# Part 2 of a two-part transformer block: experts weighted by pairs on VectorE and summed in a tree on GpSimd, with new orders on three engines

## The reference

```python
rw = _gating(hidden_states, sim_matrix, gates)            # [b, t, 16], a weight for each expert
q = jnp.einsum('bte,bted->btd', rw, jnp.einsum('btc,ecd->bted', hidden_states, q_proj))
k = jnp.einsum('bte,bted->btd', rw, jnp.einsum('btc,ecd->bted', hidden_states, k_proj))
v = jnp.einsum('bte,bted->btd', rw, jnp.einsum('btc,ecd->bted', hidden_states, v_proj))
scores = where(causal, jnp.einsum('bqd,bkd->bqk', q, k) * scale, -inf)
attn = jnp.einsum('bqk,bkd->bqd', jax.nn.softmax(scores, axis=-1), v)
mixed = attn[:, :, None, :] * rw[..., None]
return jnp.einsum('bted,edc->btc', mixed, o_proj)
```

## Time and profile before

| | before |
|---|---|
| median of 3 runs | 1579.34 us (1577.45 to 1579.94) |
| the profiled execution's own time | 1579.77 us |
| its span (first to last instruction) | 1577.8 us |
| TensorE busy, whole span | 1406.7 us, 89% |
| VectorE busy | 1044.1 us, 66% |
| ScalarE busy | 846.3 us, 54% |
| GpSimd busy | 467.7 us, 30% |

### The profile page before, as it was taken

One profiled execution on the slowest core, in us unless ns is written; L12 is line 12 of the kernel. 1 busy time (PEld: TensorE's weight loads), 2 busy tenths in 40 slices (PEclk: granted clock), 3 DMA queues, 4 the chain that ended last, 5 costly groups with the idle time before them and its releaser, 6 DMA issues.

```text
span 1577.8 us, 55685 instructions
## 1 busy us (share of the span) xinstructions
PE 1406.7 (89%) x24914; PEld 1044.7 (66%) x24914; DVE 1044.1 (66%) x1599; ACT 846.3 (54%) x1753; POOL 467.7 (30%) x496
## 2 busy tenths in 40 slices
PE   1599999999999999999999999999963687878876
PEld 0257777777777777777777777777762355555555
DVE  5576666766766666676766667676317577777776
ACT  2056565565655655665556556556633345545543
POOL 4202323233343323324232333412232222222221
PEclk9689999999999999999999999999985899999999
DMA  3101010110101001010110101010002000000000
GB/s 102 45 17 43 7 38 19 27 33 13 43 13 33 23 23 35 11 43 13 33 24 22 43 3 43 13 33 3 3 8 48 2 6 8 8 6 9 8 8 10
DMA packets 37037, 36.43 MB, mean 23 GB/s; under 512 B 14272, under 2 KB 24256, under 8 KB 36800
## 3 DMA queue, kind: packets, MB, share of 16 engines
q1 hardware_dynamic: 36288, 32.62, 8.7%
q10 hardware_dynamic: 512, 0.26, 0.1%
HBM read 5.33 MB, written 2.10 MB: 5 GB/s over the span
## 4 chain that ended last, share of the span: by engine, by line
PE 76%; DVE 9%; POOL 6%; issue 4%; ACT 4%; SPq 1%; DMA 0%; DVEq 0%; POOLq 0%; ACTq 0%
PE att_ps L511 31%; PE st_ps L495 15%; PE ring_ps L562 14%; PE ring_ps L549 4%; POOL sum_P L470 3%; PE qkv_ps L645 3%; POOL sum_P L473 2%; DVE part L1253 2%; PE ring_ps L542 2%; PE ring_ps L583 2%; DVE part_max L1078 1%; PE ring_ps L575 1%; ACT by_A L899 1%; DVE nm L1299 1%; PE t_ps L688 1%
## 5 line engine op out<-in xcount | busy, mean ns | idle before, releaser
L1078 DVE TENSOR_REDUCE part_max<-ring_ps 128x2 f32<-128x1024 f32 x512 | 625.5, 1224 | 353.3 <-PE ring_ps L562 344.4
L511 PEld LDWEIGHTS att_ps<-v_sb,pT 128*64 128x64 f32 x16384 | 632.2, 138 | 145.4 <-issue 30.1
L511 PE MATMUL att_ps<-v_sb,pT 128*64 128x65 f32 x16384 | 651.1, 222 | 2.4 <-issue 2.4
L799 ACT ACTIVATE pT<-st_ps 128x512 f32<-128x512 f32 x1024 | 553.8, 608 | 160.8 <-PE st_ps L495 153.8
L495 PE MATMUL st_ps<-qa,ka 98*64 98x512 f16 x2048 | 398.4, 387 | 0.0
L562 PE MATMUL ring_ps<-ka,qa 96*64 96x512 f16 x2048 | 313.5, 386 | 27.6 <-DMA ka<-split 19.1
L645 PE MATMUL qkv_ps<-ew_split,x2T 128*128 128x384 f16 x768 | 156.9, 337 | 25.7 <-issue 18.8
L807 ACT ACTIVATE raw_attn<-att_ps 128x260 f32<-128x260 f32 x128 | 49.5, 387 | 205.7 <-PE att_ps L511 205.7
L495 PEld LDWEIGHTS st_ps<-qa,ka 98*64 98x64 f16 x2048 | 115.4, 110 | 61.2 <-issue 10.2
L562 PEld LDWEIGHTS ring_ps<-ka,qa 96*64 96x64 f16 x2048 | 96.5, 113 | 66.5 <-issue 33.1
L470 POOL TENSOR_TENSOR sum_P<-by_A 128x576 f32<-128x576 f32 x32 | 44.9, 1404 | 256.1 <-ACT by_A L899 256.1
(11 more groups left out here) (193 smaller groups left out, 1310.8 us busy)
## 6 DMA issues: line engine op xcount, KB each, us to landing
qa<-split SPq DMA_DIRECT2D x192, 64.0 KB, 2.0
ka<-split SPq DMA_DIRECT2D x192, 64.0 KB, 2.0
resid<-in_L_attn_x SPq DMA_DIRECT2D x4, 512.0 KB, 7.3
out<-yo SPq DMA_DIRECT2D x32, 64.0 KB, 1.5
qa<-shift_rows ACTq DMA_DIRECT2D x64, 4.0 KB
wkv_sb<-in_L_attn_Wkv SPq DMA_DIRECT2D x1, 512.0 KB, 5.3
ew<-in_L_ffn_q_proj SPq DMA_DIRECT2D x1, 512.0 KB, 5.8
ew<-in_L_ffn_k_proj SPq DMA_DIRECT2D x1, 512.0 KB, 7.6
```

The costliest lines, as they stand in the source:

```text
L511: mm = pe.matmul(att_ps[q0:q0 + TILE_COLS, qt * DV1:(qt + 1) * DV1], pT[:, blk % 2, kt, qt * P + q0:qt * P + q0 + TILE_COLS], v_sb[:, j % ...
L799: act.activation(pT[:, blk % 2, kt, :], st_ps[:, c % ST_BANKS, :], ACT.Exp).then_inc(exp_ok, 1)
L1078: dve.tensor_reduce(part_max[:, which % 2, 2 * quarter + m // 2, m % 2, :], pair.rearrange("p (n k) -> p n k", n=2), AX.X, ALU.max, negate ...
```

## The change

VectorE no longer chains. For a pair it does one tensor_tensor over 2 x 192 elements: the PSUM bank times the two weights, broadcast, into a new SBUF tensor `prod[P, 2, 16, 192]`, which takes ScalarE's products too. GpSimd adds all sixteen in place: 4 + 4 experts (768 elements) three times, then 384, then 192 into `qkv`. The chain, `part`, `by_A`, `sum_P` and together(m) go. The order of steps changes on TensorE, ScalarE and VectorE, and the waits on `rest_ps` with it.

```diff
@@ GpSimd
             for m in range(B * NT):
-                pool.wait_ge(weighted_A, 2 * len(PAIRS_A) * (m + 1))
+                into = prod[:, m % 2, :, :]
+                pool.wait_ge(weighted_A, 6 * m + 4)
+                pool.wait_ge(weighted_V, 5 * m + 2)
+                pool.tensor_tensor(into[:, 0:4, :], into[:, 0:4, :], into[:, 4:8, :], ALU.add).then_inc(added_P, 1)
+                pool.wait_ge(added_P, OPS_P * m + 1)
+                pool.wait_ge(weighted_A, 6 * (m + 1))
+                pool.wait_ge(weighted_V, 5 * m + 3)
+                pool.tensor_tensor(into[:, 0:4, :], into[:, 0:4, :], into[:, 8:12, :], ALU.add).then_inc(added_P, 1)
+                pool.wait_ge(added_P, OPS_P * m + 2)
+                pool.wait_ge(weighted_V, 5 * (m + 1))
+                pool.tensor_tensor(into[:, 0:4, :], into[:, 0:4, :], into[:, 12:16, :], ALU.add).then_inc(added_P, 1)
+                pool.wait_ge(added_P, OPS_P * m + 3)
+                pool.tensor_tensor(into[:, 0:2, :], into[:, 0:2, :], into[:, 2:4, :], ALU.add).then_inc(added_P, 1)
+                pool.wait_ge(added_P, OPS_P * m + 4)
                 if m >= 2:
-                    pool.wait_ge(weighted_V, OPS_V * (m - 1))
-                pool.tensor_tensor(sum_P[:, m % 2, :, :], by_A[:, m % 2, 0:3, :], by_A[:, m % 2, 3:6, :], ALU.add).then_inc(added_P, 1)
-                for n in (1, 2):
-                    pool.wait_ge(added_P, 3 * m + n)
-                    pool.tensor_tensor(sum_P[:, m % 2, 0, :], sum_P[:, m % 2, 0, :], sum_P[:, m % 2, n, :], ALU.add).then_inc(added_P, 1)
+                    pool.wait_ge(v2_ok, m - 1)
+                    pool.wait_ge(lo2, 2 * (m - 1))
+                pool.tensor_tensor(qkv[:, m % 2, :], into[:, 0, :], into[:, 1, :], ALU.add).then_inc(added_P, 1)
@@ TensorE: outputs(m), qk_transposes(m), values2(m)
                 if live(m + 1):
                     pe.wait_ge(mx_ok, m + 2)
+                if live(m + 2):
+                    pe.wait_ge(qkt_ok, m + 3)
...
-                if live(m - 2):
-                    pe.wait_ge(mx_ok, m - 1)
+                if live(m - 1):
+                    pe.wait_ge(mx_ok, m)
...
-                if live(m + 1):
-                    pe.wait_ge(qkt_ok, m + 2)
+                pe.wait_ge(qkt_ok, m + 1)
@@ TensorE: order of a step
                 outputs(m - 4)
                 project(m, 0)
                 project(m, 1)
+                project(m, 2)
+                p_transposes(m - 2)
+                project(m, 3)
+                project(m, 4)
+                values2(m - 2)
+                project(m, 5)
                 qk_transposes(m - 1)
-                p_transposes(m - 2)
-                project(m, 2)
+                m_transposes(m - 3)
+                project(m, 6)
                 scores2(m - 1)
-                project(m, 3)
-                values2(m - 2)
-                project(m, 4)
-                m_transposes(m - 3)
-                for pair in (5, 6, 7):
-                    project(m, pair)
+                project(m, 7)
@@ ScalarE: high_parts(m) and the order of a step
-                act.wait_ge(weighted_V, OPS_V * (m + 1))
+                act.wait_ge(added_P, OPS_P * (m + 1))
...
+                weighted(m, 0)
+                weighted(m, 2)
+                p_copy(m - 2)
                 high_parts(m - 1)
-                weighted(m, 0)
+                weighted(m, 4)
                 qk_copy(m - 1)
-                p_copy(m - 2)
-                weighted(m, 2)
+                m_copy(m - 3)
                 softmax2(m - 1)
-                weighted(m, 4)
-                m_copy(m - 3)
@@ VectorE: weighted(m, pair) and the order of a step
+                if pair == PAIRS_V[0] and m >= 2:
+                    dve.wait_ge(added_P, OPS_P * (m - 1))
+                dve.tensor_tensor(prod[:, m % 2, 2 * pair:2 * pair + 2, :],
+                                  qkv_ps[:, (8 * m + pair) % QKV_BANKS, 0:6 * DE].rearrange("p (e d) -> p e d", e=2),
+                                  rw_all[:, m, 2 * pair:2 * pair + 2].unsqueeze(2).to_broadcast([P, 2, 3 * DE]),
+                                  ALU.mult).then_inc(weighted_V, 1)
...
-                low_parts(m - 1)
                 add_tokens(m - 4)
                 weighted(m, 1)
                 p_copy(m - 2)
-                maxima2(m - 1)
                 weighted(m, 3)
+                low_parts(m - 1)
                 mixed(m - 2)
                 weighted(m, 5)
                 m_low(m - 3)
                 weighted(m, 6)
+                maxima2(m - 1)
                 weighted(m, 7)
-                together(m)
```

More of the change, by code:

```diff
@@ L56 @@
 PAIRS_V = (1, 3, 5, 6, 7)
-OPS_V = 2 * len(PAIRS_V) + 1
-CHAIN_V = ((0, None), (0, 0), (0, 1), (0, 2), (0, 3), (0, 4), (1, None), (0, 5), (1, 6), (0, 7))
+OPS_P = 5
 EARLY = 3
@@ L202, in block_kernel @@
         eow_split = sb("eow_split", [P, 2, E // 2, C], F16)
-        by_A = sb("by_A", [P, 2, 2 * len(PAIRS_A), 3 * DE])
-        sum_P = sb("sum_P", [P, 2, 3, 3 * DE])
-        part = sb("part", [P, 2, 3 * DE])
+        prod = sb("prod", [P, 2, E, 3 * DE])
         qkv = sb("qkv", [P, 2, 3 * DE])
@@ L642, in project @@
                     else:
-                        pe.wait_ge(weighted_V, OPS_V * then + 2 * (PAIRS_V.index(of) + 1))
+                        pe.wait_ge(weighted_V, len(PAIRS_V) * then + PAIRS_V.index(of) + 1)
                 for k, (x_part, w_part) in enumerate(SPLIT_PRODUCTS):
@@ L896, in weighted @@
                     if m >= 2:
-                        act.wait_ge(added_P, 3 * (m - 2) + 1)
+                        act.wait_ge(added_P, OPS_P * (m - 1))
                 for e in (2 * pair, 2 * pair + 1):
-                    act.activation(by_A[:, m % 2, 2 * PAIRS_A.index(pair) + e % 2, :], expert_out(m, pair, e), ACT.Copy,
+                    act.activation(prod[:, m % 2, e, :], expert_out(m, pair, e), ACT.Copy,
                                    scale=rw_all[:, m, e:e + 1]).then_inc(weighted_A, 1)
```

## The result

The changed kernel takes 1629.08 us (median of 4, 1624.65 to 1629.97), the one before 1578.39 us in the same comparison: ratio 1.0315, 95% interval 1.0293 to 1.0336. It is slower by about 50 us, as forecast in direction and inside the range; the forecast of 1612 us is 17 us short. The profiled execution took 1624.65 us, with a span of 1622.7 us; before it was 1577.8 us.

A forecast was written before the change was run, and what follows sets the result against it. No engine is full; a ring of waits around the engines bounds each tile. Start +2.9, periods +27.9 and tail -2.6 make +28.2 us, 1607.5 us as a median; +5 us for TensorE's clock gives 1612 us, range 1597 to 1634.

The forecast's parts named there:

- The ring: Waits once around the engines, through weighted(7), GpSimd's last adds, low_parts, mixed and the q and k transposes; mean 10.47 us.
- the hold: On VectorE, low_parts' first instruction is blocked until GpSimd's running first add ends: 1.15 us more in each tile.
- 9.71 + d: Tile period in us if low_parts are not blocked; d is maxima2's time, 0.29 (v = 0) to 1.225 (v = 7).
- The port: VectorE instructions with two SBUF inputs wait for GpSimd's add to end; low_parts blocked, 1.15 us a tile, mean period 11.6.
- The first rival: GpSimd's add does not block low_parts on VectorE: -8.2 us, 1571 us; chance 0.10.
- TensorE's clock: Idle 3.0 to 3.7 us ahead of the q and k transposes, about one in four tiles begins at 1.2 GHz: +5 us.
- Q: Start of a tile's three transposes of q and k on TensorE, the mark for periods; before, 10.63 us apart.
- The second rival: TensorE's clock falls in every tile: 1607.5 + 23 = 1631 us; chance 0.12.
- my own case: low_parts blocked by GpSimd's first add, some tiles begun at 1.2 GHz: between 1598 and 1624 us; chance 0.71.
- The third rival: weighted(m, 3) comes over 1.1 us later, so low_parts go before GpSimd's first add: 1575 to 1590 us; chance 0.05.
- Start and tail: Up to the q and k transposes of tile 2, +2.9 us; from those of tile 31 to the end, -2.6 us.
- The fourth rival: VectorE is the bound, and its 1.75 us less in a tile gives -56 us, 1524 us; chance 0.02.

The follow-up runs named there:

- e2b_port_fill: The changed kernel with GpSimd's first add waiting for low_parts and pair 5 projected four times over: 1576.31 us, 0.9992 of the kernel before.
- e1_port: The changed kernel with one wait more, GpSimd's first add of a tile waiting for low_parts of the tile before: 1579.88 us.
- e3_add: The kernel before with one more GpSimd add of 768 elements in each tile, on spare SBUF that nobody reads: 1649.17 us.
- e3_memset: The kernel before with one more GpSimd instruction in each tile, a memset of 2304 elements on spare SBUF: 1577.88 us.
- e2_fill: The changed kernel with pair 5 of each tile but the first projected six times over, same result: 1608.56 us.
- e4_orders: The kernel before with the change's new orders and waits on TensorE, ScalarE and VectorE, but the old sums: 1546.69 us.
- e6_short: The changed kernel with GpSimd's first add waiting for low_parts and a tree whose last adds are small: 1547.70 us.

## Why the prediction was right, and where it was short

1. **The ring and its period without the hold, 9.71 + d: right.** e2b_port_fill has 10.12 to 11.06 against 10.00 to 10.94, 0.12 us more in each tile. Of this, 0.09 us is the way from weighted(7) to `qkv`, 3.71 us for 3.62. Prices of all new instructions were within 1.5%.
2. **The port: right, and shown from both sides.** Taken away in the changed kernel (e1_port), put alone into the kernel before (e3_add), and without GpSimd's reads (e3_memset). Size: 1.10 us a tile for 1.15 (the prediction's own terms, 2.34 and 1.17, give 1.17). This error and that of the ring run against each other, so that a tile with the hold came within 0.08 us of the forecast was in part luck.
3. **The first rival** (port not held, 1571) is refuted as a forecast by L1259; as a reckoning of a kernel without the hold it was near (1576 in e2b_port_fill).
4. **TensorE's clock: the term that was mis-sized.** The prediction let one in four of 29 tiles begin at 1.2 GHz, at 0.8 us each, +5 us. In the trace 19 of the 29 tiles from Q of tile 2 to Q of tile 31 are over 0.3 us longer than forecast, each with a mean granted clock of 0.83 to 0.89; the nine at 0.99 to 1.00 are within 0.1 us of the forecast, and one at 0.85 is shorter than forecast (point 5). Together the 29 take 355.0 us (1249.01 to 1604.04) for 336.1, 1.0 us more for each slow tile. So the price was near and the count was wrong. e2_fill takes that away: 20.5 us by the medians, 16.7 between the two profiled executions (the changed kernel's was the fastest of its four). The second rival, a fall in every tile, was nearer than my own case: 1631 us. Its counter-argument holds in part. The hole behind a slow tile is shorter (2.51 us at v = 5, where a full one has 3.05), and in 7 of 19 cases the next tile is a full one (11.48, 12.51, 11.74, 12.92); so it stayed at two in three.
5. **The third rival happened in a few tiles, and mostly not as written.** In five tiles weighted(3) came after the end of the adds by so much that low_parts' first instruction was free. In four the add then started with the first instruction or up to 0.03 us behind it, and held the second for its full length:

```profile
1320.62 1.90 POOL L466 TENSOR_TENSOR prod<-prod 128x768 f32<-128x768 f32 x1 [0.52 <-DVE prod L1250]
1320.62 0.23 DVE L1259 SCALAR_TENSOR_TENSOR qs<-qkv,qs 128x64 f16<-128x64 f32 x1
...
1320.76 1.90 DVE L1261 SCALAR_TENSOR_TENSOR qs<-qkv,qs 128x128 f16<-128x128 f32 x1
```
In one, both were through first, and the tile lasted 11.65 us in place of 11.95:

```profile
1504.63 0.23 DVE L1259 SCALAR_TENSOR_TENSOR qs<-qkv,qs 128x64 f16<-128x64 f32 x1
...
1504.77 0.28 DVE L1261 SCALAR_TENSOR_TENSOR qs<-qkv,qs 128x128 f16<-128x128 f32 x1
1504.91 1.81 POOL L466 TENSOR_TENSOR prod<-prod 128x768 f32<-128x768 f32 x1 [0.81 <-DVE prod L1250]
```
From the end of L480 to Q it is 4.2 us in the first case, 2.7 in the second and 3.65 in an ordinary tile (1417.94 to 1421.59). So what the prediction priced as a gain was a loss in four of five. In ten more tiles the add started 0.07 to 0.53 us ahead of low_parts in place of 0.56, and their first instruction took 1.37 to 1.82 us. All fifteen lie in tiles with a granted clock of 0.83 to 0.87, and e2_fill, with the full clock, has none: a late add is one way in which the low clock costs time.
6. **Start and tail.** Start +0.6 us for +2.9 (Q of tile 2 at 1249.01 against 1248.40). The two steps behind Q of tile 0 took 20.8 us, forecast 21.0; the difference lies ahead of them. Q of tile 0 came at 1228.19 for 1230.35, as GpSimd's first add began at 1218.62 for 1220.9, and Part 2's first projection at 1213.9 (1216.2 before). Part 1 is the same in both kernels, and in the traces of all runs that projection begins anywhere from 1213.0 to 1216.2, so this gain is luck. Tail, from Q of tile 31 at 1604.04 to the end of the span: 18.7 us, forecast 18.6; before 21.2. The sum in the trace: 0.62 + 46.81 - 2.56 = 44.9 us of span.
7. **The fourth rival** (VectorE's share decides, 1524) is refuted: from 1250 to 1520 us VectorE is busy 177.3 of 270 us, 210.3 before, and the kernel is slower.

Where the change's 50 us are, by the runs: with the full clock and no hold it would be level with the kernel before (e2b_port_fill); the hold is 32 us; the clock 20 us of the rest. And the new orders by themselves are worth -31 us (e4_orders), which the tree's 3.7 us behind weighted(7) eat up: with 1.8 to 2.3 us in their place e6_short is level with e4_orders.

## What to carry to other kernels

Give GpSimd adds only where no VectorE instruction with two SBUF inputs stands on the path at that time, or make it wait: an add that nobody needed yet cost 1.0 to 1.3 us a tile, and one more wait on GpSimd took 49 us off. Where the sum of many parts ends a ring, add the early parts first and leave little behind the last one (1.8 to 2.3 us in place of 3.7 gave 32 us). Price a loss on a ring through TensorE with what its clock does in the longer hole; here that added 0.6 (20.5 to 32.3 us) and 0.8 (32 to 39 us) of the loss itself.

## What was not expected of the hardware

- A GpSimd memset of 2.02 us does not hold a VectorE instruction with two SBUF inputs, an add of 1.80 us does (0.23 against 1.50 us).
- The clock's share of a loss: 1.28 us a tile of hold in the kernel before became 2.3 us a tile, as the granted clock went from 1.00 in the like stretch of the memset's kernel to 0.91. TensorE's waits ahead of the slow transposes there were 2.1 us in one piece, with another of 1.2 us in the tile.
- Of the two low_parts instructions either can be the one that is held; the second, with its add 0.03 us behind the start of the first, took 1.89 us.
